# Triangular inverses in the middle stage: TensorE products of two sequences side by side on four quadrants

## Reference

```python
def step(W, qkv):
    q_t, k_t, v_t = qkv
    y_t = jnp.einsum('bds,bs->bd', W, q_t)
    pred = jnp.einsum('bds,bs->bd', W, k_t)
    err = pred - v_t
    W = W - TTT_LR * err[:, :, None] * k_t[:, None, :]
    return (W, y_t)
...
x = x + 0.5 * ffn(layernorm(x))
x = x + scan_of_step(layernorm(x))     # keys, values, queries with 64, 256, 64 features
x = x + 0.5 * ffn(layernorm(x))
```

## Time and profile before

| | us |
|---|---|
| Median of 3 runs (2513.54 to 2515.21) | 2514.35 |
| Profiled execution, device time | 2515.57 |
| Its span, first to last instruction | 2513.8 |
| TensorE busy in the span | 2473.0 (98%) |
| VectorE busy | 1972.8 (78%) |
| ScalarE busy | 1812.3 (72%) |
| GpSimd busy | 1563.0 (62%) |
| Mean granted TensorE clock, share of full speed | 0.999 |

### The profile page before, as it was taken

The page is one execution under the profiler, slowest core; times in us unless marked ns, Lnnn a source line. Parts: engine busy times, 40 slices in busy tenths (PEclk is TensorE's granted clock), DMA queues, the critical chain, the costliest instruction groups (busy, mean ns, idle before and its releaser), DMA issues. The chain is left out here.

```text
span 2513.8 us, 80296 instructions
## 1 busy us (share of the span) xinstructions
PE 2473.0 (98%) x29664; PEld 2224.4 (88%) x29664; DVE 1972.8 (78%) x6501; ACT 1812.3 (72%) x5224; POOL 1563.0 (62%) x1799
## 2 busy tenths in 40 slices
PE   8999999999999999999999999999999999999999
PEld 7889989999999999998777889999999989999998
DVE  7788888877877887777655888777877788888886
ACT  6777777777777777776454777777777777777775
POOL 6566667666666666665212677666666667666665
PEclk9999999999999999999999999999999999999999
DMA  3121111013000000005100000000003100000000
GB/s 127 35 86 52 40 58 56 27 29 115 15 3 2 3 2 28 2 22 192 36 19 32 5 3 2 2 2 2 2 2 118 41 3 19 19 19 19 19 19 27
DMA packets 75958, 82.21 MB, mean 33 GB/s; under 512 B 37553, under 2 KB 61873, under 8 KB 74417
## 3 DMA queue, kind: packets, MB, share of 16 engines
q1 hardware_dynamic: 74272, 75.61, 9.2%
q10 hardware_dynamic: 1296, 1.46, 0.2%
HBM read 49.53 MB, written 26.74 MB: 30 GB/s over the span
## 5 line engine op out<-in xcount | busy, mean ns | idle before, releaser
L642 POOL TENSOR_TENSOR pr<-pr,rden 128x384 f32<-128x384 f32 (+1 forms) x480 | 409.9, 871 | 276.0 <-DVE rden L1811 270.8
L856 ACT ACTIVATE pr<-pr,nb 128x192 f32<-128x192 f32 (+1 forms) x1024 | 438.0, 429 | 170.6 <-DVE nb L1802 170.6
L1165 PE MATMUL bank<-h2T,w 128*128 128x256 f32 x1344 | 386.0, 287 | 2.4
L1166 PE MATMUL bank<-h2T,w 128*128 128x256 f32 x1344 | 376.8, 280 | 0.0
L1167 PE MATMUL bank<-h2T,w 128*128 128x256 f32 x1344 | 376.7, 280 | 0.0
L1802 DVE CUSTOM_DVE_ANT_0 pr<-bank,maskb,r 128x192 f32<-128x192 f32 (+1 forms) x1024 | 346.9, 392 | 26.6 <-POOL r L637 11.8
L684 POOL TENSOR_TENSOR uTl<-t,uTh 128x256 fp32r<-128x256 f32 x288 | 218.3, 763 | 181.7 <-ACT uTh L956 148.4
L1165 PE MATMUL bank<-wqkv,hT 128*128 128x512 f32 x768 | 304.4, 396 | 1.8 <-DVE nb L1802 1.8
L1166 PE MATMUL bank<-wqkv,hT 128*128 128x512 f32 x768 | 302.5, 394 | 0.0
L1167 PE MATMUL bank<-wqkv,hT 128*128 128x512 f32 x768 | 299.7, 390 | 0.0
L1906 DVE SCALAR_TENSOR_TENSOR t<-bank,b,t 128x256 f32<-128x256 f32 (+1 forms) x384 | 184.5, 480 | 107.9 <-POOL uTl L684 46.9
(11 more groups left out here) (255 smaller groups left out, 7114.1 us busy)
## 6 DMA issues: line engine op xcount, KB each, us to landing
wqkv<-wqkv_split SPq DMA_DIRECT2D x18, 512.0 KB, 6.3
w<-w_split SPq DMA_DIRECT2D x3, 2816.0 KB, 9.7
Y<-in_x SPq DMA_DIRECT2D x8, 512.0 KB, 7.7
stt<-stt SPq DMA_DIRECT2D x256, 3.0 KB
out<-Y SPq DMA_DIRECT2D x8, 512.0 KB, 3.6
h<-out SPq DMA_DIRECT2D x7, 512.0 KB, 3.8
out<-h SPq DMA_DIRECT2D x7, 512.0 KB, 3.0
stt<-stt SPq DMA_DIRECT2D x192, 0.0 KB
```

Source lines behind the costliest of these rows:

```text
L642: e.tensor_tensor(probs(j, t), probs(j, t), rden[:, 2 * j:2 * j + 2].unsqueeze(2).to_broadcast([P, 2, w]), ALU.mult).then_inc(pn_done, 1 i ...
L856: last = e.activation(probs(j, t)[:, g, :], probs(j, t)[:, g, :], ACT.Exp, bias=nb[:, hd:hd + 1], scale=-1.0, accum_out=den[:, hd:hd + 1])
L1165: e.matmul(out, left[0], right[0], start=first, stop=False)
L1166: e.matmul(out, left[0], right[1], start=False, stop=False)
```

## The change

The change is in the order of work and in the place of sequence 1 in the array; the same products are made.

- **Quadrants.** `block` takes the half that it reads and the half that it writes apart. For sequence 1 the product writes the other half, so that `mx[1]` and `invT[1]` are kept with their halves exchanged, and the update writes back into the plain half. Sequence 0 stays on the diagonal quadrants, sequence 1 uses the other two in products and updates. The turned updates of both stay on the diagonal.
- **Order on TensorE.** In a level the 8 products of both sequences alternate, then the 8 updates of both, then the turned update of 0 and that of 1. Each of these joint groups waits for both sequences. The values of sequence 1 are spread over levels 0 and 1, and the transposes for the next pair stand between products and updates of levels 2 and 3.
- **VectorE.** `mid_start(p, 1)` makes the exchanged `invT[1]` in two halves. `n_up` is left to ScalarE. The order in a level is inv 0, inv 1, invT 0, invT 1.
- **ScalarE.** It reads `n_up` and `n_quad` out of the bank (`kk_read`), those of sequence 1 between the copies of the two products of level 0, with one tile of `mid_h` ahead of them. The other three tiles go behind level 1.
- **GpSimd.** `out_rstd` moves one level later.

The core of the diff (the functions `mid_zT` on both engines only get their k as arguments, and `mid_h` a range of tiles):

```diff
@@ ScalarE, mid_pair
+                def kk_read(i):
+                    e.wait_ge(t_g[i], at(t_g[i], 2 * p + 1))
+                    e.activation(n_up[i], cut(bank[KK_BANK[i]][:, :], NT)[:, :, 0:64], ACT.Copy, scale=TTT_LR).then_inc(t_g[i], 1)
+                    e.activation(n_quad[i][0:64, :, :], cut(bank[KK_BANK[i]][0:64, :], NT)[:, :, 64:P], ACT.Copy, scale=TTT_LR).then_inc(t_q[i], 1)
...
+                if more:
+                    mid_h(p + 1, 0)
+                kk_read(0)
+                product_read(0, 0)
+                if more:
+                    mid_h(p + 1, 1, 0, 1)
+                kk_read(1)
+                product_read(0, 1)
+                for l in range(1, LV):
+                    for i in pair:
+                        product_read(l, i)
+                    if more and l == 1:
+                        mid_h(p + 1, 1, 1, NT)
+                    elif more and l in (2, 3):
+                        mid_zT(p + 1, l - 2, 0, 1)
@@ TensorE, mid_keys and mid_levels
-                mid_v(p, 1)
...
+            def block(bk, c, half, left, right, src=0, dst=0):
+
+                rows, cols = ROWS[half ^ src], ROWS[half ^ dst]
+                return e.matmul(bank[bk][cols, 64 * c:64 * c + 64], left[rows, c, 0:64], right[rows, c, 0:64], start=True, stop=True)
...
+                def product(l, c, half, i):
+                    return block(LP_BANK[i], c, half, m_up[i][l % 2] if l else m_first[i], inv[i], 0, i)
+
+                def update(c, half, i):
+                    return block(LU_BANK[i], c, half, invT[i], mx[i], i, 0)
...
+                def products(l):
+                    for i in pair:
+                        product_ready(i, l)
+                    for c in range(NT):
+                        for half in range(2):
+                            m0 = product(l, c, half, 0)
+                            m1 = product(l, c, half, 1)
+                    m0.then_inc(t_p_ps[0], 1)
+                    m1.then_inc(t_p_ps[1], 1)
...
                 for l in range(LV):
...
+                    if l < 2:
+                        mid_v(p, 1, 2 * l, 2 * l + 1)
+                    products(l)
+                    if l < 2:
+                        mid_v(p, 1, 2 * l + 1, 2 * l + 2)
+                    elif more and l < 4:
+                        mid_zT(p + 1, l - 2, 0, 1)
+                    updates(l)
+                    turned_update(l, 0)
+                    turned_update(l, 1)
@@ VectorE, mid_start (replaces mid_masks)
+            def mid_start(p, i):
+                kk = cut(bank[KK_BANK[i]][:, :], NT)[:, :, 0:64]
+                if i == 0:
+                    m = e.tensor_tensor(start[0], kk.unsqueeze(2).to_broadcast([P, NT, 3, 64]),
+                                        mask_first.unsqueeze(1).to_broadcast([P, NT, 3, 64]), ALU.mult)
+                else:
+                    e.tensor_tensor(start[1][:, :, ::2, :], kk.unsqueeze(2).to_broadcast([P, NT, 2, 64]),
+                                    mask_first[:, ::2, :].unsqueeze(1).to_broadcast([P, NT, 2, 64]), ALU.mult)
+                    for half in range(2):
+                        m = e.tensor_tensor(invT[1][ROWS[1 - half], :, :], kk[ROWS[half], :, :],
+                                            mask_first[ROWS[half], 1:2, :].to_broadcast([64, NT, 64]), ALU.mult)
+                m.then_inc(t_g[i], 1)
+                e.wait_ge(t_g[i], at(t_g[i], 2 * p + 1))
+                e.tensor_tensor(start[i][:, :, 0:2, :], eye64.unsqueeze(1).unsqueeze(1).to_broadcast([P, NT, 2, 64]),
+                                start[i][:, :, 0:2, :], ALU.subtract).then_inc(t_i[i], 1)
...
+                mid_start(p, 0)
+                mid_a(p, 0)
+                mid_start(p, 1)
                 mid_levels(p)
@@ VectorE, mid_levels
                 for l in range(LV):
                     for i in pair:
+                        mid_update(p, l, i)
+                    for i in pair:
+                        mid_turned_update(p, l, i)
                     if l < 2:
                         mid_v(p, 1, l)
```

More of the change, by code:

```diff
@@ L1051, in transformer, with mid_h @@
                     sequence(L, B - 1, (L, B - 2), None if last else (L + 1, 0))
-            def mid_h(p, i):
+            def mid_h(p, i, first=0, end=NT):
                 k = 2 * p + i
-                e.wait_ge(t_rs, at(t_rs, 2 * k + 2))
-                if p:
-                    e.wait_ge(t_zt_ps[i], at(t_zt_ps[i], 2 * p))
-                for t in range(NT):
+                if first == 0:
+                    e.wait_ge(t_rs, at(t_rs, 2 * k + 2))
+                    if p:
+                        e.wait_ge(t_zt_ps[i], at(t_zt_ps[i], 2 * p))
+                for t in range(first, end):
                     m = e.activation(hn[i][:, t, :], x_mid[p % 2][i][:, t, :], ACT.Identity, bias=off1[:, i, 1, t:t + 1], scale=rs1[:, i, 1, t:t + 1])
-                m.then_inc(t_h[i], 1)
+                if end == NT:
+                    m.then_inc(t_h[i], 1)
             def mid_xz(p, i):
@@ L1068, in mid_xz, with mid_zT @@
                 m.then_inc(t_xz, 1)
-            def mid_zT(p, i):
-                for k in range(KT):
+            def mid_zT(p, i, *ks):
+                for k in ks:
                     e.wait_ge(t_zt_ps[i], at(t_zt_ps[i], 2 * p + k + 1))
@@ L1520, in transformer, with mid_zT @@
                     mid_v(0, 0, 0, 2)
-                    mid_zT(0, 1)
+                    mid_zT(0, 1, 0, 1)
                     mid_v(0, 0, 2, NT)
-            def mid_zT(p, i):
+            def mid_zT(p, i, *ks):
                 e.wait_ge(t_h[i], at(t_h[i], p + 1))
-                for k in range(KT):
+                for k in ks:
                     if i:
@@ L1587, in mid_keys @@
                 m.then_inc(t_a_ps, 1)
-                mid_v(p, 1)
-            def blocks(bk, lo, left, right):
-                for c in range(NT):
-                    for half in range(2):
-                        m = e.matmul(bank[bk][ROWS[half], lo + 64 * c:lo + 64 * c + 64], left[ROWS[half], c, 0:64], right[ROWS[half], c, 0:64],
-                                     start=True, stop=True)
-                return m
-            def mid_levels(p):
-                for l in range(LV):
-                    for i in pair:
-                        if l == 0:
-                            e.wait_ge(t_v[0], at(t_v[0], 2 * p + i + 1))
-                        else:
-                            e.wait_ge(t_m[i], at(t_m[i], (LV - 1) * p + l))
-                        e.wait_ge(t_i[i], at(t_i[i], TI * p + (2 * l if l else 1)))
-                        blocks(LP_BANK[i], 0, m_up[i][l % 2] if l else m_first[i], inv[i]).then_inc(t_p_ps[i], 1)
-                    for i in pair:
-                        e.wait_ge(t_p[i], at(t_p[i], (LV + 1) * p + l + 1))
-                        e.wait_ge(t_i[i], at(t_i[i], TI * p + 2 * l + 1))
-                        if l == 0:
-                            e.wait_ge(t_g[i], at(t_g[i], 2 * p + 2))
-                            e.wait_ge(t_q[i], at(t_q[i], 2 * p + 1))
-                        blocks(LU_BANK[i], 0, invT[i], mx[i]).then_inc(t_i_ps[i], 1)
-                        if l == 0:
-                            e.wait_ge(t_a[i], at(t_a[i], p + 1))
-                        blocks(LUT_BANK[i], 0, mx[i], invT[i]).then_inc(t_i_ps[i], 1)
-                    if p + 1 < B // 2 and l in (2, 3):
-                        mid_zT(p + 1, l - 2)
@@ new lines, in mid_a, with mid_update @@
+            def mid_a(p, i):
+                e.wait_ge(t_a_ps, at(t_a_ps, p + 1))
+                e.tensor_tensor(a_up[i], cut(bank[A_BANK[i]][:, :], NT), over_tiles(mask_a, NT), ALU.mult).then_inc(t_a[i], 1)
+            def mid_update(p, l, i):
+                e.wait_ge(t_i[i], at(t_i[i], TI * p + (2 * l if l else 1)))
+                e.wait_ge(t_i_ps[i], at(t_i_ps[i], TI * p + 2 * l + 1))
+                rows = ROWS[0] if l == LV - 1 else slice(0, P)
+                e.tensor_tensor(inv[i][rows, :, :], inv[i][rows, :, :], cut(bank[LU_BANK[i]][rows, 0:256], NT), ALU.subtract).then_inc(t_i[i], 1)
@@ new lines, in mid_turned_update @@
+            def mid_turned_update(p, l, i):
+                e.wait_ge(t_i[i], at(t_i[i], TI * p + 2 * l + 1))
+                e.wait_ge(t_i_ps[i], at(t_i_ps[i], TI * p + 2 * l + 2))
+                if l < LV - 1:
+                    e.tensor_tensor(invT[i], invT[i], cut(bank[LUT_BANK[i]][:, 0:256], NT), ALU.subtract).then_inc(t_i[i], 1)
+                else:
+                    for half in range(2):
+                        rows, held = ROWS[half], ROWS[half ^ i]
+                        m = e.tensor_tensor(wholeT[i][rows, :, rows], invT[i][held, :, :], cut(bank[LUT_BANK[i]][held, 0:256], NT), ALU.subtract)
+                    m.then_inc(t_i[i], 1)
@@ L2217, in mid_levels @@
             def mid_levels(p):
+                mid_a(p, 1)
                 for l in range(LV):
                     for i in pair:
[L2220 to L2223 removed]
```

78 lines of the change are left out of this document (38 added, 40 removed).

## The result

| | before | after |
|---|---|---|
| Median of 5 runs, us | 2515.21 (2513.54 to 2517.38) | 2526.1 (2524.9 to 2528.8) |
| Ratio, 95% interval | 1 | 1.0044 (1.0032 to 1.0056) |
| Profiled execution, its span | 2513.8 | 2523.1 |
| Mean granted clock | 0.999 | 0.996 |

The changed kernel is slower by 0.44%, 10.9 us. It lies 2.1 above the upper end of the range, 7.7 above the forecast.

A forecast was written before the change was run, and what follows sets the result against it. It took a plain level as bound by TensorE's issue, turning into waits for copies and subtractions. Profiled 2515.57 + 1.7 for steps + 2.3 for the clock gave 2519.6; the median, 1.2 below, 2518.4 us, range 2514.5 to 2524.

The forecast's parts named there:

- rival 3: Joint groups: only two quadrants run at once, each group takes 0.94, 18.8 more, 2537 us; chance 0.06.
- rival 2: Levels: TensorE's issue stays the bound, so the kernel gets faster by 5.3 us, to 2509.0; chance 0.06.
- Level 0's 2.53: Level 0, product to update, with ScalarE's copies, key bank reads and a `mid_h` tile: 2.53 us, against 1.17 before.
- levels 1 and 3: Product to update: 1.67 us in level 1 with a tile of values, 1.65 in level 3 with transposes.
- update to product ahead of level 1: Level 0's update to level 1's product: 1.45 of issue plus 1.2 for an uncovered tile of values, 2.6 us.
- the plain level, 3.06: A level without tiles or transposes: 1.46 product to update plus 1.6 to the next product, 3.06 us against 3.03.
- the clock, 2.3: Pauses ahead of level 0: granted clock falls in 2.5 of 4 pairs at 0.9 each, 2.3 us, between 0 and 6.8.
- rival 4: More clock lost, by a fall fully on the path in each pair or a second one: 2522.9 to 2526; chance 0.14.
- The start: From a pair's first product of keys with keys to level 0's first product: 5.63 us, 0.13 earlier than before.
- the end: From level 4's update to the first error product: 3.74 us.
- level 0 of the last pair: Product to update in level 0 without the `mid_h` tile: 2.04 us.
- 1.7 as forecast: Middle stage's steps over four pairs: +0.22 for each of three pairs, +1.07 for the last, together +1.7 us.

The follow-up runs named there:

- diag: Changed kernel with both sequences on the two diagonal quadrants, order of work and waits kept: 2541.21 us, ratio 1.0095.
- waits: Changed kernel with only the order of TensorE's semaphore waits rewritten, the one released last written first: 2521.88 us, ratio 1.0032.
- fill: Changed kernel plus 20 unread TensorE transposes per pair in the pause ahead of level 0: 2525.05 us, ratio 1.0039.
- copies: Changed kernel with ScalarE's copies of both level 0 products in a row, key bank reads ahead, `mid_h` tile behind: 2523.38 us, ratio 1.0037.
- tiles: Changed kernel with all four tiles of values of sequence 1 ahead of level 0 again: 2523.35 us, ratio 1.0032.
- cross: `order` with the turned update of sequence 0 and update of sequence 1 issued in turns, VectorE in the changed kernel's order: 2508.89 us, ratio 0.9966.
- order: Changed kernel's quadrants, but each sequence waits for itself; values ahead of level 0, copies in a row, VectorE sequence by sequence: 2513.86 us, ratio 0.9987.
- order_diag: `order` with sequence 1 back on the two diagonal quadrants: 2513.97 us, ratio 0.9993.

## Why the prediction was wrong

**Right: what bounds, and the overlap.** A level did turn from issue into handovers. Four quadrants run at once (a joint group 0.49 against 0.48; rival 3 would have been `diag`). The gain in issue turned into waiting for copies and subtractions, so rival 2 did not come in this order. Level 0's 2.53 measured 2.47 in `waits`, where no further semaphore instruction stands behind the last release; levels 1 and 3 are 1.69 and 1.65 (1.67, 1.65), update to product ahead of level 1 is 2.61 (2.6). (The prediction calls the 16 records of a group 16 products; they are eight products of two records each. It counts so on both sides, and no sum changes.)

**The step that failed: the plain level, 3.06.** Its terms took TensorE's handover from traces in which one sequence waits for itself, 0.44 and 0.46, and carried them over to a group that waits for both. It measured 3.35. The forecast left out that a joint group's waits are instructions of TensorE's own queue, and that the order in which they are written decides what lies behind the last release. `waits`, which changes that order alone, gives 3.08. Over the four pairs it is about 3.6.

**Mis-sized: the clock, 2.3.** In this execution it came as forecast in kind: each pair has the pause of 2.55 and then a granted clock of 0.50. I had 2.5 falls of 0.9. There are four stretches, one of 6.83, and they cost more. By steps without a fall (5.80 + 2.87 + 2.61 + 1.69 + 1.71 + 1.76 + 1.71 + 1.65 + 1.71 + 1.65 + 3.92 = 27.08, and 26.46 for the last pair) the sum would be 107.7 in place of 112.6: 4.9, within the bound of 6.8 that rival 4 named. Its price was read too low, since after level 0's update TensorE has its issue and the values on the path: this step takes 4.77 in pair 0 in place of 2.61. `fill`, without falls, gives 4.3 for it. Both are figures of single executions.

**Mis-sized: start and end.** The start 5.80 in place of 5.63, of which 0.09 are waits (5.71 in `waits`); the end 3.92 in place of 3.74, four times 0.18; level 0 of the last pair 2.21 in `waits`, partly at half clock, in place of 2.04. Together 1.2, and 0.1 in small steps.

The parts add up: 1.7 as forecast, 3.6 + 1.3, and 4.9 for the clock are 11.5 of stage sum, where 11.6 was measured. Against the forecast's 1.7 + 2.3 this is 7.6 more, and 2518.4 + 7.6 is 2526.0; the median is 2526.1. That these two meet so closely is luck. The 4.9 comes from one execution, the fastest of the five; the stage's 11.6 are 10.9 in the medians; and the 1.2 that the forecast took off for the median would be 0.4 by the five runs.

**The range.** Rival 4 had the clock alone at 2522.9 to 2526, and the handovers had no rival of their own: 1 us for ten steps of 0.1 "partly cancelling". They did not cancel: the waits' order made several of them longer and none shorter but one (level 2, by 0.09).

**What stays open.** How the clock falls are spread. `waits` and `copies` have the same pause of about 2.5 ahead of level 0 in all four pairs, and two and three of these have a fall. `tiles` has one fall, and its pause, inside level 0, is 2.2 (1.7 in the last pair). `diag` has 1.95 ahead of level 0, and all four of its pairs have a fall. The length of the pause alone doesn't decide. Open too is what of the gain of `cross` over `order` is the joint group and what is VectorE's order.

## What to carry to other kernels

Where two chains take turns on an engine, putting them in step takes away the cover that each gives the other; save issue only where the second one is ready by itself (`cross`), or only give it free quadrants (`order`, whose gain over `order_diag` shows in the stage alone). For a group that waits for several semaphores, let the instruction itself carry the wait that is released last (here the one written first), and have the others worked off ahead of it. Price every semaphore instruction from the one that is released last on, that one included. A step read from a trace holds only with the number of waits that it has there.

## What the runs showed of the hardware

- On TensorE a semaphore instruction of its own has a record of 51 ns if it need not wait itself; two start 0.11 us apart, and the weight load follows the last by 0.08. Where the last release meets the first of two such instructions, product to update is 0.19 longer than with the load carrying that wait (1.65 and 1.46, `waits`); where it meets the first of four, 0.40 (2.87 and 2.47).
- Groups of 64 x 64 products on disjoint quadrants overlap without being interleaved in the program, and their MATMUL records start out of the program's order: 0.25 to 0.29 from one to the next in `order`, 0.48 on the same quadrants. The Trainium skill, "TensorEngine Tiling (Array Packing)", section Overview, gives up to two times for such operands. The trace of a joint group agrees (0.49 for two groups' work, 0.48 for one's before), but the whole level gains only 0.34 of 3.03 by it, and 0.46 in `cross`.
- The granted clock can fall to 0.50 where TensorE has hardly paused: its longest pause in that pair is 0.59 in `order`, and 0.77 in the pair of `cross` that has a fall. In `order`, busy time by stretch in the error products of pair 1, and the stretch ahead of it:

```profile
1259.20:1262.60 3.40, 3.40 (x10) 1.76 (x9) 2.23 (x12) 1.60 (x4) 0.00 (x0) 0.50 0.00 0
...
1251.00:1259.20 8.20, 7.43 (x200) 6.59 (x199) 5.58 (x15) 3.75 (x9) 0.00 (x0) 1.00 0.01 2
```

TensorE is busy for all of the first and for 7.43 of the 8.20 ahead of it. No run here says why it fell.
